# One-hots of four low parts: one comparison of two tensors in place of four comparisons with a scalar of each partition

## The reference, cut to what matters

```python
def rgcn_conv(x, src, dst, etype, W, root, bias):
    n = x.shape[0]
    seg = dst * R + etype
    x_src = x[src]
    agg = jax.ops.segment_sum(x_src, seg, num_segments=n * R)
    cnt = jax.ops.segment_sum(jnp.ones((src.shape[0],), x.dtype), seg, num_segments=n * R)
    agg = jnp.where(cnt[:, None] > 0, agg / jnp.maximum(cnt, 1.0)[:, None], 0.0)
    agg = agg.reshape(n, R, -1)
    return jnp.einsum('nrd,rdk->nk', agg, W) + x @ root + bias
```

## Time and profile before

| | |
|---|---|
| time, median of 3 runs | 5596.16 us (5591.11 to 5609.0) |
| time of the profiled execution | 5605.28 us |
| span of its instructions | 5603.4 us |
| busy: PE, PEld, DVE, ACT, POOL | 79%, 56%, 47%, 57%, 57% |
| stretch in which batches are made | 1336.0 to 3507.5 us |

### The profile page before, as it was taken

The page is one execution under the profiler, slowest core; times in us unless marked ns, Lnnn a source line. Parts: engine busy times, 40 slices in busy tenths (PEclk is TensorE's granted clock), DMA queues, the critical chain, the costliest instruction groups (busy, mean ns, idle before and its releaser), DMA issues.

```text
span 5603.4 us, 86440 instructions
## 1 busy us (share of the span) xinstructions
PE 4453.9 (79%) x30196; PEld 3138.0 (56%) x30196; DVE 2632.7 (47%) x7852; ACT 3177.9 (57%) x4502; POOL 3190.0 (57%) x3114
## 2 busy tenths in 40 slices
PE   2688999996666666666566666599999979999998
PEld 1466666663344334434343434477777757777776
DVE  5888882113656666566666666212222221222222
ACT  2566661002444444444444444399888978888887
POOL 5000000004777777777777777477777746777775
PEclk7799999997777878788887888799999989999999
DMA  3223324654555656565555556567776766666664
GB/s 96 87 113 143 121 113 157 241 217 128 145 168 145 175 146 173 142 174 152 160 166 147 169 146 173 186 224 259 255 262 219 260 228 204 207 212 207 212 208 157
DMA packets 629486, 994.44 MB, mean 177 GB/s; under 512 B 359122, under 2 KB 511324, under 8 KB 625212
## 3 DMA queue, kind: packets, MB, share of 16 engines
q1 hardware_dynamic: 159412, 552.80, 27.7%
q0 software_dynamic: 146944, 302.80, 19.0%
q10 hardware_dynamic: 322696, 133.28, 8.8%
HBM read 715.99 MB, written 272.14 MB: 176 GB/s over the span
## 4 chain that ended last, share of the span: by engine, by line
PE 37%; POOL 23%; issue 8%; DVE 4%; DMA 3%; ACT 1%; SPq 1%; ACTq 0%; DVEq 0%; POOLq 0%
PE couple_bank L1530 27%; POOL messages L1481 23%; PE bank L1496 5%; DMA slices<-relations_d 1%; DMA messages<-table,src_rows 1%; PE bank L1568 1%; SPq L1401 1%; DVE ring L1839 1%; PE bank L1554 1%; DVE scaled L1832 1%; DVE type_scaled L1832 1%; DMA type_scaled<-node_hot 1%; PE bank L1544 1%; PE couple_bank L1512 1%; ACT lots L1318 0%
## 5 line engine op out<-in xcount | busy, mean ns | idle before, releaser
L1481 POOL DMA_INDIRECT messages<-table,src_rows x2320 | 2415.9, 1041 | 820.7 <-issue 652.9
L1318 ACT CAST lots<-slices 128x1024 fp32r<-128x1024 fp8e4 (+1 forms) x1750 | 1674.4, 1027 | 260.2 <-PE couple_bank L1530 216.1
L1530 PE MATMUL couple_bank<-lots,pieces 128*128 128x512 f32 x6860 | 1715.6, 403 | 16.5 <-ACT lots L1318 16.3
L1647 ACT CAST stage<-couple_bank 128x980 fp8e4<-128x980 f32 x896 | 841.0, 985 | 1132.1 <-PE couple_bank L1512 978.4
L1530 PEld LDWEIGHTS couple_bank<-lots,pieces 128*128 128x128 f32 x6860 | 1256.7, 189 | 325.9 <-ACT lots L1318 57.4
L1496 PE MATMUL bank<-group_hot,messages 128*128 128x120 bf16 x9084 | 692.4, 234 | 399.4 <-DMA messages<-table,src_rows 359.1
L1496 PEld LDWEIGHTS bank<-group_hot,messages 128*128 128x128 bf16 x9084 | 584.5, 107 | 662.6 <-issue 615.6
L1481 POOL DMA_INDIRECT messages<-table,rel_rows x708 | 688.7, 973 | 326.3 <-issue 173.6
L1793 DVE TENSOR_TENSOR ring<-ring,bank 128x120 f32 x354 | 99.1, 280 | 1464.8 <-PE bank L1496 1461.4
L1512 PE MATMUL couple_bank<-rel_hot,lo_dense_hot 128*128 128x490 bf16 x1792 | 597.6, 446 | 196.1 <-ACT stage L1647 178.3
L1462 POOL IOTA iota_rel_i<- 128x120 int32 (+1 forms) x4 | 1.7, 469 | 1185.7 <-DMA table<-typed_rows 1185.7
(11 more groups left out here) (272 smaller groups left out, 3851.2 us busy)
## 6 DMA issues: line engine op xcount, KB each, us to landing
slices<-relations_d SPq DMA_DIRECT2D x210, 768.0 KB
relations_d<-stage ACTq DMA_DIRECT2D x336, 240.0 KB
adjacency_d<-adjacency SPq DMA_DIRECT2D x15, 4704.0 KB, 14.5
adjacency<-adjacency_d SPq DMA_DIRECT2D x15, 4704.0 KB, 15.3
slices<-relations_d SPq DMA_DIRECT2D x70, 832.0 KB
pieces<-dense SPq DMA_DIRECT2D x42, 896.0 KB, 11.0
messages<-table,src_rows POOLq DMA_INDIRECT x2320
dense<-table_halves SPq DMA_DIRECT2D x49, 640.0 KB
```

Source lines behind the costliest of these rows:

```text
L1318: return copy(to, of_slice[:, :, first:end, :])
L1481: pool.indirect_dma_start(messages_in(i)[:, t, 0:ROWS[v]], None, GATHERED[v], bass.IndirectOffsetOnAxis(ap=rows[:, e:e + 1], axis=0)).then ...
L1530: mm = pe.matmul(bank[DENSE_BANKS[K % 2]][:, 0:DENSE_COLS], pieces[M % PIECE_RING][:, tile % PIECE_TILES, half * P:(half + 1) * P], lots[l ...
L1647: act.copy(to, from_banks, saturate=False).then_inc(rel_evicted, 1)
```

## The change

`dense_onehots` makes the four one-hots of the low parts of a batch by one DVE operation, which compares two tensors: the row `iota16`, read four times, and the four codes, each read 128 times over (a step of 0 in the innermost dimension). Before, four operations compared `iota16` with a scalar of each partition. The four comparisons that make `rel_hot` stay as they are. What the batch writes, and the semaphores around it, are the same.

```diff
             def dense_onehots(b):
                 if b >= HOT_RING:
                     vec.wait_ge(rel_psum, (b - HOT_RING + 1) * BATCH // 2)
+                codes = slice(b * BATCH, (b + 1) * BATCH)
+                vec.tensor_tensor(lo_dense_hot[:, b % HOT_RING, :, :], iota16[:, :].unsqueeze(1).broadcast_to([P, BATCH, P]),
+                                  lo_dense[:, codes].unsqueeze(2).broadcast_to([P, BATCH, P]), ALU.is_equal)
                 for m in range(BATCH):
-
-                    vec.tensor_scalar(lo_dense_hot[:, b % HOT_RING, m, :], iota16[:, :], lo_dense[:, b * BATCH + m:b * BATCH + m + 1], None, ALU.is_equal)
                     op = vec.tensor_scalar(rel_hot[:, b % HOT_RING, m, :], iota_rel[:, :], rel_dense[:, b * BATCH + m:b * BATCH + m + 1], None, ALU.is_equal)
                 op.then_inc(rel_hot_made, 1)
```

## The result

Over 20 runs of each, the changed kernel takes 5616.07 us and the one before 5604.21: 11.9 us longer, a ratio of 1.0023 (95% interval 1.0016 to 1.0030). The forecast was 51 us longer. (The 5596.16 us of the front are the median of the first three runs.)

The account below looks back on a forecast made before the run. POOL's issue of gathers was taken to bound the first convolution; 54 us added by the new comparison less 3 for the removed ones made 51 us longer, 5647 us as the median, range 5605 to 5690.

Parts of the forecast that it names:

- What bounds the kernel: First relational convolution: its 2184 us are as long as POOL takes to issue 1596 gathers, without idle time to spare.
- DVE's own time: Per batch, 0.64 us of short comparisons go and 0.61 us come (one of 690 ns); batch length unchanged within 0.03 us.
- What the new comparison adds: Gathers beginning within the long two-tensor comparison wait for its end: 188 hits of 288 ns, 54 us longer.
- What the removed comparisons gave POOL to wait for: Gathers beginning within the removed short comparisons had waited little: 3 us saved, between 2.4 and 40.
- The four `rel_hot` comparisons: Same number and length, standing closer together; gathers meet one more often but over a shorter time: costed at nothing.
- It runs at the rate of L1768: Rival: the new comparison takes some 415 ns, adding 15 us less 3, for 5608 us; chance 6%.
- The toll per operation: Rival: each DVE operation costs POOL a fixed 42 ns, so 1344 fewer give back 57 us, 5539; chance 5%.
- The new comparison leaves gathers alone: Rival: gathers do not wait for it, so only the removed ones count: -3 us, 5593, at most -40; chance 6%.
- The loss of a further turn behind the long comparison: Rival: a gather that waited loses again to the next `rel_hot` comparison, 49 us more, 5696; chance 7%.
- The gathers miss it: Rival: two in three of the expected gathers fall outside the new comparison; 15 us remain, 5611; chance 6%.
- the law: A gather beginning within a two-tensor SBUF operation on DVE loses that operation's remaining time, less some 0.1 us (measured: 0.13).

Follow-up runs that it names:

- e1: The changed kernel with the long low-part comparison made for the first three batches only, later batches reusing them: 5541.06 us, 0.9881 of the kernel before.
- e8: The kernel before, its short comparisons alone reading 5 rows of 26 numbers, the `rel_hot` ones as they were: 5570.67 us, ratio 0.9928.
- e9: The kernel before, short comparisons reading 5 rows of 26 and placed first in a batch, `rel_hot` ones in their old form: 5631.96 us, ratio 1.0050.
- e3: The changed kernel with two comparisons of 256 columns in place of the one of 512: 5564.29 us, 0.9929 of the kernel before.
- e7: The kernel before, with both short and `rel_hot` comparisons reading 5 rows (of 26 and 98 numbers), order unchanged: 5534.77 us, ratio 0.9872.
- e5: The changed kernel with four two-tensor comparisons of 128 columns in place of the one of 512: 5574.06 us, 0.9946 of the kernel before.
- run 86: Not a follow-up run: "run" is a row of back-to-back comparisons, and 86 counts the delayed gathers among 170.

## Why the prediction was wrong

*What bounds the kernel: right.* POOL's issue bounds the stage; its idle time stayed at 491 us, and the change in the gathers' durations (11.4 us) is the change in the time.

*DVE's own time: right.* 684 ns measured for 690, a batch takes 1.85 us in the mean before and after, and PE's waits for `rel_hot` grew by 4.3 us without effect.

*What the new comparison adds: right in its mechanism and nearly in its direct size.* 146 of 176 gathers that met it were delayed, 49.9 us, for 188 and 54. They were fewer than worked out but lost more each, 0.34 us for 0.29, so that the sum came this near is in part luck. Taken out (e1) it is worth 75 us; with it, 13 us more are lost behind `group_hot`.

*What the removed comparisons gave POOL to wait for: this step failed.* "I take 3 us", between 2.4 and 40, was worked out from what a gather loses that begins within a short comparison itself, and there it holds: 3.9 us in the trace. Taken out, they are worth 64 us. They cost through the comparisons behind them: with the short ones there, gathers lost 78.5 us behind `rel_hot`, without them 7 to 11.

*The four `rel_hot` comparisons: the same failure, from the other side.* "I cost that at nothing" was false by 67 us. Two ways into it are shown. One is turns lost in a row behind `rel_hot`: 88 gathers with 46.6 us in the kernel before, 4 with 4.0 after, none in e8. The other is that more gathers lose a single turn there, 0.09 to 0.12 us each: 267 with 31.8 us in the kernel before, 83 with 7.2 after, and in e8, where no turns are lost in a row, 350 with 40. So of the 64 us, some 35 go when the short ones no longer hold POOL or wait for it (e8) and some 30 more when they are gone (e1). Why the short ones do that, I can only argue: see the last section. The sum also had no term for `group_hot`, where 24 us were added. When a waiting gather loses several turns stays open; e9 refutes the condition I had proposed.

*The rivals.* No rival was the answer. "It runs at the rate of L1768" is refuted by the 684 ns. The toll per operation, the one that ended faster, is refuted by e3. "The new comparison leaves gathers alone", which is what the Trainium skill's inference ("SBUF — State Buffer", section "Who interferes with whom") would make of it, is refuted by the 49.9 us. The loss of a further turn behind the long comparison was not seen at its price of 49 us: 4 of the 146 gathers, 2.9 us. "The gathers miss it" gave nearly the measured time, 5611, for a reason that the trace refutes.

The range, 5605 to 5690, did hold 5616, since it took in cases with a small gain; the forecast of 25 to 90 us did not. The error was to let every gather fall anywhere: for what is added that was good enough, but the removed comparisons and POOL wait for each other (see below). That this is what ties their places together is argued, not shown.

## What to carry to other kernels

Where a queue on GpSimd bounds a stage, price a DVE operation not by its own duration but by how long it holds the gathers, and price a removed one by an experiment without it: taking it out moves everything behind it. A comparison of two tensors in SBUF cost nearly as the square of its length (49.9 us in one piece, 25.4 in two), so try it in pieces; but four pieces, 18.7 us, made the whole kernel slower than two. A comparison with a scalar was had without any hold by laying out the source as 5 rows of 98 against a destination of 490: 464 ns in place of 343 on DVE. With both kinds of comparison so, 71 us came off the kernel (e7), where the long comparison in two halves (e3) gave 41.

## What the runs showed that I had not expected

DVE waits for gathers as well. In the kernel before, 291 short comparisons took over 0.06 us longer than their median, like this one, which ended 0.02 us after the gather; 257 of them ended within 0.04 us after one:

```profile
1354.34 0.99 POOL L1481 DMA_INDIRECT messages<-table,src_rows  x1 [0.30 <-issue]
...
1354.84 0.51 DVE L1777 TENSOR_SCALAR lo_dense_hot<-iota,lo_dense 128x128 bf16<-128x128 f16 x1
1355.00 0.48 DVE L1778 TENSOR_SCALAR rel_hot<-iota_rel,rel_dense 128x490 bf16<-128x490 f16 x1
```

The long ones do it too: in the changed kernel 341 `rel_hot` comparisons took over 0.06 us longer than their median, and all of them ended 0.10 to 0.12 us after a gather. In e7, with both kinds in rows, no comparison did. So a run of such comparisons comes into step with POOL: it goes on when a gather ends, and 0.43 us later (0.30 of issue and the 0.13 of the law) the next gather asks, at a fixed point of the run. In e1 this shows by place: of 170 gathers that met the first or second `rel_hot` comparison of a back-to-back run 86 were delayed, of 223 that met a later one none. That this stepping is what the short comparisons upset is argued from these counts, not shown.

One gather can wait for five DVE operations in a row (48 gathers in e9), once even for nine (e5): the two engines don't take turns.
